# Gated cross-attention and experts: scores on four 32-row tiles with a bank each, two chunks per score block, both exponentials ahead of the key copy

## The reference, cut to what matters

```
B, S, T, H, NH, HD = 32, 56, 1500, 256, 16, 16
q = layernorm(x) @ Wq.T + bq          # (B, 56, 256)
k = ctx @ Wk.T + bk                   # (B, 1500, 256)
v = ctx @ Wv.T + bv
scores = clip(q . k / 4, -50, 50), masked positions -50     # per head
probs = softmax(scores)
x = x + tanh(g_xattn) * layernorm(rs * (probs @ v @ Wo.T + bo)) * gamma + beta (gated)
logits = layernorm(x) @ w_router      # top 2 of 8
x = x + tanh(g_ffn) * sum_e w_e * relu(layernorm(x) @ w_fc[e])**2 @ w_proj[e]
```

## Time and profile before

| | |
|---|---|
| median of 3 runs | 1195.04 us (1194.09 to 1195.85) |
| the profiled execution, its own time | 1202.38 us |
| its span on the core | 1200.3 us |
| mean granted clock of PE | 0.981 |
| PE busy | 1130.6 us, 94% |
| weight loads busy | 1082.1 us, 90% |
| DVE busy | 862.1 us, 72% |
| ACT busy | 664.2 us, 55% |
| instructions of PE: matmuls, weight loads | 24824 each |

### The profile page before, as it was taken

How to read it: one execution, slowest core, us unless ns; L and a number is a source line. 1 busy time by engine, 2 the same in 40 slices (tenths; PEclk the granted TensorE clock), 3 DMA queues, 4 the chain that set the end, 5 groups by cost and what they waited for, 6 DMA issues and landing times.

```text
span 1200.3 us, 56000 instructions
## 1 busy us (share of the span) xinstructions
PE 1130.6 (94%) x24824; PEld 1082.1 (90%) x24824; DVE 862.1 (72%) x2003; ACT 664.2 (55%) x846; POOL 156.8 (13%) x186
## 2 busy tenths in 40 slices
PE   4799999999999999999999999999999999969884
PEld 4799999999999999999999999999999999968874
DVE  4467776777777776777777777777777777757677
ACT  1466565655556565656565556656565656534432
POOL 0000100010010101010111101010101101023431
PEclk9799999999999999999999999999999999989998
DMA  4223132222323233323222232323321222124306
GB/s 153 74 74 91 57 93 79 85 76 77 91 88 91 67 87 93 80 63 94 83 86 68 89 91 88 87 71 87 93 78 50 79 61 71 30 54 120 90 25 169
DMA packets 59487, 98.57 MB, mean 82 GB/s; under 512 B 14514, under 2 KB 42034, under 8 KB 59250
## 3 DMA queue, kind: packets, MB, share of 16 engines
q1 hardware_dynamic: 49538, 79.55, 23.9%
q10 hardware_dynamic: 6832, 8.92, 2.1%
q0 software_dynamic: 2880, 6.53, 1.5%
HBM read 70.32 MB, written 24.71 MB: 79 GB/s over the span
## 4 chain that ended last, share of the span: by engine, by line
PE 86%; issue 5%; DVE 5%; DMA 2%; POOL 1%; ACT 1%; SPq 0%; DVEq 0%; POOLq 0%; ACTq 0%
PE v_ps L601 22%; PE k_ps L604 21%; PE sc_ps L627 20%; PE o_ps L642 13%; PE k_ps L659 1%; PE sc_ps L544 1%; PE sc_ps L545 1%; PE k_ps L666 1%; PE sc_ps L546 1%; PE v_ps L692 1%; DVE acc L1509 1%; DVE h_sq L1438 1%; DVE acc L1452 1%; POOL rstd L460 0%; PE k_ps L805 0%
## 5 line engine op out<-in xcount | busy, mean ns | idle before, releaser
L897 ACT ACTIVATE prob<-sc_ps,m_bias 125x896 f32<-125x896 f32 x384 | 377.9, 1009 | 329.7 <-PE sc_ps L627 329.3
L601 PE MATMUL v_ps<-wv_hi,c_hi 64*125 64x256 f32 x1520 | 312.0, 285 | 2.7 <-DVE c_lo L1066 2.6
L604 PE MATMUL k_ps<-c_hi,wk_hi 64*128 64x500 f32 x760 | 306.8, 404 | 0.0
L601 PE MATMUL v_ps<-wv_lo,c_hi 64*125 64x256 f32 x1520 | 302.1, 279 | 0.0
L601 PE MATMUL v_ps<-wv_hi,c_lo 64*125 64x256 f32 x1520 | 301.9, 278 | 0.0
L604 PE MATMUL k_ps<-c_lo,wk_hi 64*128 64x500 f32 x760 | 294.0, 387 | 0.0
L604 PE MATMUL k_ps<-c_hi,wk_lo 64*128 64x500 f32 x760 | 293.2, 386 | 0.0
L1075 DVE TENSOR_TENSOR vst<-v_ps,rowv 125x512 f32<-125x512 f32 x191 | 131.3, 687 | 184.9 <-PE v_ps L601 184.9
L1277 DVE TENSOR_SCALAR prob<-prob 125x896 f32<-125x896 f32 x384 | 235.5, 626 | 21.3 <-ACT prob L897 21.1
L601 PEld LDWEIGHTS v_ps<-wv_hi,c_hi 64*125 64x125 f32 x1520 | 227.0, 185 | 16.6 <-issue 5.7
L627 PE MATMUL sc_ps<-q_hi,kh 64*125 64x224 f32 x1536 | 231.1, 268 | 7.1 <-ACT prob L897 7.1
(11 more groups left out here) (193 smaller groups left out, 1664.3 us busy)
## 6 DMA issues: line engine op xcount, KB each, us to landing
raw<-in_ctxT SPq DMA_DIRECT2D x96, 500.0 KB, 3.8
slot_rows<-zero_row SPq DMA_DIRECT2D x112, 132.0 KB, 3.7
rows<-slot_rows SPq DMA_DIRECT2D x32, 132.0 KB, 2.1
w_raw<-in_we ACTq DMA_DIRECT2D x16, 256.0 KB, 5.1
rec<-inv_scratch SPq DMA_DIRECT2D x64, 56.0 KB
expert_out<-expert_rows SPq DMA_DIRECT2D x6, 448.0 KB, 7.3
xq<-in_x ACTq DMA_DIRECT2D x16, 112.0 KB, 4.0
xr<-in_x ACTq DMA_DIRECT2D x16, 112.0 KB, 3.7
```

Source lines behind the costliest of these rows:

```text
L601: v_last = pe.matmul(v_ps[0:TC, j * D:(j + 1) * D], c_s[v_rows, cs], w_m[v_rows, k, :], start=begin and j == 0, stop=end, skip_group_check ...
L604: k_last = pe.matmul(k_ps[:, half, 0:TG], w[k_rows, k, ws], c_m[k_rows, :], start=begin, stop=end)
L897: act.activation(prob[0:TC, c % PB, :].rearrange("p (c n) -> p c n", c=2), sc_ps[0:TC, 2 * (c % 2):2 * (c % 2) + 2, 0:NH * S // 2], ACT.Ex ...
```

## The change

The scores go to four row tiles of 32 rows (two heads each, QH = 2, QW = 32), each with its own bank of sc_ps; a matmul has 2 x 56 = 112 moving columns, and 24 of them make a chunk in place of 12. A chunk takes half of each of the four banks, so two chunks share all four: `scores` now does both in one go, waits for all exponentials before it, and signals both at its end. q_hi, q_lo and the mask hmask are half as wide. In PE's order the scores of a pair of chunks stand ahead of a half's two parts, which now follow each other. On ACT both exponentials of a half stand ahead of the key copy, on DVE the first clip ahead of the value copy. `pv` finds a head's columns by a new formula; its matmuls stay.

```diff
-CST = (P, NE, HS, KD, KD, PW, NE, NE * NE, CAP // SL, NU, 1, 2 * NS)
+CST = (P, NE, QH, KD, KD, PW, NE, NE * NE, CAP // SL, NU, 1, 2 * NS)
...
-            def scores(i, c):
+            def scores(i, c0):
...
-                wait(pe, exp_done, n - 1)
-                cs = slice(c % GC * TC, (c % GC + 1) * TC)
-                for m in range(KD):
-                    for term, (k, q) in enumerate(((kh, q_hi), (kh, q_lo), (kl, q_hi))):
-                        for r in range(2):
-                            rows = slice(r * HW, (r + 1) * HW)
-                            last = pe.matmul(sc_ps[0:TC, 2 * (c % 2) + r, m * HS * S:(m + 1) * HS * S],
-                                             k[rows, g % 2, m, cs], q[rows, b, m, :, :], start=term == 0, stop=term == 2)
-                last.then_inc(scores_done, 1)
+                wait(pe, exp_done, n)
+                for c in (c0, c0 + 1):
+                    cs = slice(c % GC * TC, (c % GC + 1) * TC)
+                    for m in range(KD):
+                        at = (c % 2 * KD + m) * QH * S
+                        for term, (k, q) in enumerate(((kh, q_hi), (kh, q_lo), (kl, q_hi))):
+                            for r in range(ST):
+                                rows = slice(r * QW, (r + 1) * QW)
+                                last = pe.matmul(sc_ps[0:TC, r, at:at + QH * S], k[rows, g % 2, m, cs], q[rows, b, m, :, :],
+                                                 start=term == 0, stop=term == 2, tile_position=(r * QW, 0))
+                last.then_inc(scores_done, 2)
...
                     beside_pv(i, q, first, late, final)
+                    if first and q == 0:
+                        pe.wait_ge(v_evac, 2)
+                    scores(i, c)
                     if more:
                         kv_part(n, 0, slot, 0)
-                    scores(i, c)
-                    if more:
                         kv_part(n, 0, slot, 1)
-                    if first and q == 0:
-                        pe.wait_ge(v_evac, 2)
-                    scores(i, c + 1)
-                    if not more:
+                    else:
                         turn(0)
                     scores(i, c + 2)
                     if more:
                         kv_part(n, 1, slot, 0, freed.get(q, ()))
-                    scores(i, c + 3)
-                    if more:
                         kv_part(n, 1, slot, 1)
...
                     exps(i, 2 * u)
-                    if half == 1:
-                        exps(i, 2 * u + 1)
+                    exps(i, 2 * u + 1)
                     if not (final and q == PG - 1):
                         k_hi_evac(i * PG + q + 1, half, (q + 1) % 2)
-                    if half == 0:
-                        exps(i, 2 * u + 1)
...
+                    clip(i, 2 * u)
+                    if half == 1:
+                        clip(i, 2 * u + 1)
+                    if more:
+                        v_evac_step(i * PG + q + 1, half, (q + 1) % 2)
                     if half == 0:
-                        if more:
-                            v_evac_step(i * PG + q + 1, half, (q + 1) % 2)
-                        clip(i, 2 * u)
-                        if more:
-                            k_lo_evac(i * PG + q + 1, half, (q + 1) % 2)
                         clip(i, 2 * u + 1)
-                    else:
-                        clip(i, 2 * u)
-                        clip(i, 2 * u + 1)
-                        if more:
-                            v_evac_step(i * PG + q + 1, half, (q + 1) % 2)
-                            k_lo_evac(i * PG + q + 1, half, (q + 1) % 2)
+                    if more:
+                        k_lo_evac(i * PG + q + 1, half, (q + 1) % 2)
```

More of the change, by code:

```diff
@@ L32 @@
 HW = HS * HD
+QH = 2
+QW = QH * HD
 NE = 8
@@ L192, in gated_cross_attention_moe @@
         q_rem = sb("q_rem", [P, KD, S], scope=att)
-        q_hi = sb("q_hi", [P, 2, KD, HS, S], fp32r, scope=att)
-        q_lo = sb("q_lo", [P, 2, KD, HS, S], fp32r, scope=att)
+        q_hi = sb("q_hi", [P, 2, KD, QH, S], fp32r, scope=att)
+        q_lo = sb("q_lo", [P, 2, KD, QH, S], fp32r, scope=att)
         early = ExitStack()
@@ L611, in kv_part @@
                     v_last.then_inc(vproj_done, 1)
-            def scores(i, c):
-                n = i * PC + c
-                b, g = c // NC, c // GC
-                if c % NC == 0:
+            def scores(i, c0):
+                n = i * PC + c0
+                b, g = c0 // NC, c0 // GC
+                if c0 % NC == 0:
                     pe.wait_ge(q_ready, 4 * i + 2 * b + 2)
-                if c % GC == 0:
+                if c0 % GC == 0:
                     pe.wait_ge(k_lo, KD * (i * PG + g + 1))
-                wait(pe, exp_done, n - 1)
-                cs = slice(c % GC * TC, (c % GC + 1) * TC)
-                for m in range(KD):
-                    for term, (k, q) in enumerate(((kh, q_hi), (kh, q_lo), (kl, q_hi))):
-                        for r in range(2):
-                            rows = slice(r * HW, (r + 1) * HW)
-                            last = pe.matmul(sc_ps[0:TC, 2 * (c % 2) + r, m * HS * S:(m + 1) * HS * S],
-                                             k[rows, g % 2, m, cs], q[rows, b, m, :, :], start=term == 0, stop=term == 2)
-                last.then_inc(scores_done, 1)
+                wait(pe, exp_done, n)
[9 more added lines that the diff above has]
+                last.then_inc(scores_done, 2)
             def pv(i, c):
@@ L640, in pv @@
                     col, q = divmod(h, ST)
-                    at = (h // HS % 2 * KD + h // (2 * HS)) * HS + h % HS
+                    at = (h % (NH // KD) // QH * KD + h // (NH // KD)) * QH + h % QH
                     last = pe.matmul(o_ps[q * 32:q * 32 + VW, col * S:(col + 1) * S], vst[0:TC, c // GC % 2, c % GC, h, :],
@@ L894, in exps @@
                 n = i * PC + c
-                act.wait_ge(scores_done, n + 1)
+                act.wait_ge(scores_done, n + 2 - c % 2)
                 wait(act, pv_done, n - PB + 1)
-                act.activation(prob[0:TC, c % PB, :].rearrange("p (c n) -> p c n", c=2),
-                               sc_ps[0:TC, 2 * (c % 2):2 * (c % 2) + 2, 0:NH * S // 2], ACT.Exp,
+                at = c % 2 * KD * QH * S
+                act.activation(prob[0:TC, c % PB, :].rearrange("p (r n) -> p r n", r=ST),
+                               sc_ps[0:TC, :, at:at + KD * QH * S], ACT.Exp,
                                scale=SCALE, bias=m_bias[0:TC, bass.ds(n, 1)]).then_inc(exp_done, 1)
@@ L1110, in q_diagonal @@
             def q_diagonal(dst, b, part):
-                shape = [P, KD, HS, S]
+                shape = [P, KD, QH, S]
                 dve.tensor_tensor(dst[:, b, :, :, :], part.unsqueeze(2).to_broadcast(shape),
@@ L1544 @@
             np.tile(NE - np.arange(NE, dtype=np.float32), (P, 1)),
-            (r[:, None] % HW // HD == np.arange(HS)[None, :]).astype(np.float32),
+            (r[:, None] % QW // HD == np.arange(QH)[None, :]).astype(np.float32),
             np.asarray(L0_xattn_bk).reshape(KD, P).T, np.asarray(L0_xattn_bq).reshape(KD, P).T,
```

## The result

The changed kernel takes **1491.7 us** (median of 4 runs, 1487.35 to 1493.74) against 1194.57 (1193.16 to 1195.85) before on the same chip: ratio 1.248, interval 1.245 to 1.252, 297 us slower. I had said 1313 us in a range of 1250 to 1342: slower was right, the size was not.

A forecast was written before the change was run, and what follows sets the result against it. PE, busy 94% of the span, was taken to bound the kernel, its scores paced by weight loads. +1.08 us a block in 95 blocks (+103), +12 and +3 made +118 us: median 1195.04 to 1313 us, range 1250 to 1342.

The forecast's parts named there:

- a score group costs 0.109 us: In the scores, weight loads set the pace: a group of four 32-row matmuls costs 0.109 us, so halved columns buy nothing.
- Rival 2: In the scores, the 32-row load costs half, saving 0.054 us in each of 24 groups: 1190 us; chance 8%.
- rival 3: In the scores, four loads don't run side by side: 0.218 us a group, +249 us, 1562 us; chance 5%.
- (b): Three crossings per block between 32-row scores and 64-row projection drain PE: 0.21 us, or 0.16 from scores to projection.
- Rival 1: At scores-projection crossings, no drain between 32 and 64 rows, 0.07 to 0.09 us each: 1264 us; chance 15%.
- (a): In the projection, part 1 right behind part 0 waits for it: 0.36 us for 0.12, two parts 3.10 us.
- (c): A block's first scores, right behind PV, wait for DVE's low key rest: 0.8 us a pair, 15 pairs, +12 us.
- (d): At the start, chunk 0's scores move behind the value copy, so two parts and six groups come later: +3 us.
- The step that failed: In the scores, twice as many PE instructions are no limit: PV issues pairs at 12 ns each, four in 0.109 us need 27.

The follow-up runs named there:

- e1: The new order alone with the old 64-row tiles, against the kernel before: 1285.72 us for 1202.53, ratio 1.069.
- e5: The changed kernel with PV for only 10 of the 16 heads in each chunk: 1318.76 us, against 1204.74 for the kernel before, ratio 1.095.
- e7: The changed kernel with the first projection part moved between PV and the first scores: 1432.42 us, against 1204.74 for the kernel before, ratio 1.190.
- e2: The kernel before with 128 semaphore increments put once ahead of the second pair of sequences: 1252.59 us for 1202.53, ratio 1.039.
- e6: e5 with lines' ends moved by 192 instructions, by 96 tiny matmuls once in the second pair: 1315.5 us, ratio 1.092 to the kernel before.
- b_shift224: The kernel before with lines' ends moved by 224 instructions, by 112 tiny matmuls once in the second pair: 1206.21 us for 1204.27, ratio 1.0018.
- b_shift32: The kernel before with lines' ends moved by 32 instructions, by 16 tiny matmuls once in the second pair: 1226.4 us for 1204.74, ratio 1.019.

## Why the prediction was right and wrong

**Right: a score group costs 0.109 us.** 804.02, 804.13, 804.24: four loads of 125 columns side by side take the time of two, and neither the halved rows nor the halved moving columns buy anything. Rival 2 (half the load) and rival 3 (loads two at a time) are out, though rival 3's 1562 us is nearest to what was measured; 48 scores in 1.26 us deny its mechanism.

**Right: (b), drains.** Crossings between 32 and 64 rows are 0.20 and 0.21 us, those between 64 and 64 rows in e1 0.10 and 0.09. Rival 1 (no drain) is out. From scores to projection I had taken 0.16; it is 0.20. The Trainium skill, TensorEngine Tiling (Array Packing), section Key Properties, says that changing the tiling mode drains TensorE; these four crossings agree.

**Right, a little small: (a), the wait between parts.** 0.43 us (801.86, the last start of the row at 801.74, to 802.29) for my 0.36. With a bare load behind each drain two parts take 3.21 us for 3.10.

**(c) and (d).** (c) was worth some 8 us in e1, for 12 forecast, and nothing in the whole change (PV to scores 0.15 us in the mean): blocks of 14 us give DVE time. (d) cost 1.0 us, not 3.

**Sum without the failed step.** By medians +124 for the blocks where I had 103, and 1 for (c) and (d) where I had 15: 125 for 118. On 1195 us that is 1320, inside the range.

**The step that failed** is the sentence "Twice as many instructions are no limit: PV issues 128 load-and-matmul pairs in 1.56 us, 12 ns each, and four in 0.109 us need 27". That is the pace at which instructions already there leave the queue. It isn't the pace at which they come. The scores alone are no denser than the prediction says: 96 records in 1.26 us, 13 ns each, and PV has 6 ns. What it left out is that they now stand right behind PV, 352 records in 3.0 us and more than a line, while packets never start less than 3.3 us apart; and that 96 records more in a block take the lines' ends out of the place that `whole_lines` gave them. On the average the supply would do: a pair brought 3072 records in 6 x 10.93 us before, 21 ns each, and by medians the change wants one in 19 ns. The +150 of the means is the price of the bursts, and no rival of mine had it. The trace of before could not show the stops themselves: its gaps over 0.3 us at lines' ends are 1.4 us in all, and PV's 8.5 us of issue lie elsewhere, ten of them as gaps of some 0.66 us within PV that aren't at a line's end. What stood there to be read were 199 packets for 50985 instructions, and `whole_lines` in the program. That rival 3 came nearest to the time was luck.

**What is shown and what is not.** Shown: the lines of 256 (packets and gaps agree in two kernels); that the stops lie at their ends and last until the line's own packet has landed; that they nearly go when the count goes back and PV is thinner (e5: 12.2 us of gaps over 0.3 us at lines' ends, for 110 in the change); that they shrink when the rich stretches are parted (e7); and that the ends' place alone costs the kernel before 0.2 to 1.9%. The half clock, 227 us of the program against 47 before, comes behind the stops and goes with them; how the loss beyond the medians (150 us by the table) splits into standing (95 us more gaps) and slow steps is not exact, since a slower PE also spends fewer instructions. Open: what sets the start of a packet. It lies about one line ahead: in the change between 1.7 us before and 5.1 us after the first record of the line before it, and at the stops 2.0 us after it in the median. A fixed time per line doesn't fit: in e2 ends 1.6 to 2.5 us apart often pass with 0 to 0.6 us, since the lines between last over 8, while in the change stops of 3.6 us occur. A packet itself takes 0.98 us in the median after and 1.01 before, so the transfer is not what became longer. Open too is how the 214 us of the small tiles divide between the number of records, their bursts and the wandering ends: a multiple of 256 for the changed kernel was not tried in a form that could tell. e6 and b_shift224 say that the place matters little in some programs, b_shift32 that it matters in others.

## What to carry to other kernels

Count instructions per microsecond as a resource of their own: before splitting matmuls into smaller tiles, add up records in each stretch, and look where a line of 256 would be spent faster than the 3.3 us that lay at least between two packets here. PV did that before too, with 256 records in 1.56 us, and it was free where a line ended in its middle; with the ends at its start and end (e2) they cost some 30 us. So mind the place of the ends as well. "issue" in the list of waits, gaps in mid-run with no semaphore, and a mean that leaves its median are the signs; number the engine's records, look at the remainder by 256, and compare with the landing of the instruction queue's packets. And halving the moving columns of a matmul whose pace is set by its weight load saved nothing here, while each change of tile rows between neighbours cost 0.1 us and left a load bare.

## What the runs showed that was not expected

- One PE program, shifted by 32 instructions in 50985, runs 1.9% longer; by 192, 1.1%; by 224, 0.2%.
- A semaphore increment on PE costs 0.13 to 0.14 us in a row of them, ten times a product of PV with its load (12 ns).
- A stop of 1.3 us on PE was followed by projection steps of 0.42 us for 0.23, at a granted clock of 0.59 in that stretch, while e1, with a gap of 0.43 us between the two parts of each half, kept 0.983 in the mean.
- The Trainium skill, Runtime: NRT & Kernel Launch, section Instruction fetch mechanics, calls the fetch of instructions hidden behind their issue. In this kernel it isn't: 60 stops, 107 us.
